# Delta layer: transposed outputs joined with block products on more tiles of the array, and a new order of squares, sums, norms and value copies

## What is computed

```python
qkvz = hidden_states @ w_qkvz.T
...
yc = jax.lax.conv_general_dilated(xc, conv_w[:, None, :], (1,), [(KCONV - 1, 0)], feature_group_count=CONV_DIM, dimension_numbers=('NCH', 'OIH', 'NCH'))
yc = jax.nn.silu(yc).transpose(0, 2, 1)
q, k, v = jnp.split(yc, [KEY_DIM, 2 * KEY_DIM], axis=-1)
...
q = q * jax.lax.rsqrt(jnp.sum(q * q, -1, keepdims=True) + L2_EPS)
k = k * jax.lax.rsqrt(jnp.sum(k * k, -1, keepdims=True) + L2_EPS)
...
def step(S, xs):
    qt, kt, vt, gt, bt = xs
    S = S * jnp.exp(gt)[..., None, None]
    kv = jnp.einsum('bhk,bhkv->bhv', kt, S)
    delta = (vt - kv) * bt[..., None]
    S = S + jnp.einsum('bhk,bhv->bhkv', kt, delta)
    o = jnp.einsum('bhk,bhkv->bhv', qt * scale, S)
    return (S, o)
...
xf = o.astype(jnp.float32) * jax.nn.silu(z.astype(jnp.float32))
var = jnp.mean(xf * xf, -1, keepdims=True)
xn = xf * jax.lax.rsqrt(var + NORM_EPS) * norm_weight
return xn.reshape(B, T, VALUE_DIM) @ w_out.T
```

## Time and profile before

| | |
|---|---|
| median of 3 runs | 2417.58 us (2417.31 to 2418.69) |
| profiled execution | 2418.08 us, its span from the first to the last instruction 2416.2 us |
| mean granted TensorE clock | 0.937 |
| busy in the span | PE 2096.6 us (87%), DVE 1845.9 us (76%), ACT 1462.5 us (61%), POOL 212.9 us (9%) |

### The profile page before, as it was taken

One profiled execution on the slowest core, in us unless ns is written; L12 is line 12 of the kernel. 1 busy time (PEld: TensorE's weight loads), 2 busy tenths in 40 slices (PEclk: granted clock), 3 DMA queues, 4 the chain that ended last, 5 costly groups with the idle time before them and its releaser, 6 DMA issues. The chain is left out here.

```text
span 2416.2 us, 41501 instructions
## 1 busy us (share of the span) xinstructions
PE 2096.6 (87%) x16485; PEld 1518.6 (63%) x16536; DVE 1845.9 (76%) x3313; ACT 1462.5 (61%) x2436; POOL 212.9 (9%) x163
## 2 busy tenths in 40 slices
PE   7997448999999999999976589999999996888854
PEld 4665325776666777776664355788888874555633
DVE  4776667888888888888877835478888776588697
ACT  3664255667777767676626631577777776455355
POOL 0000100011000000111100051000000000100313
PEclk8999768999999999999988799999999997999978
DMA  3000012322322222322216355311010000200001
GB/s 159 2 1 13 13 40 57 105 81 73 93 82 83 72 80 82 108 80 73 73 45 213 138 136 175 115 32 58 23 27 6 6 18 1 81 1 2 16 1 35
DMA packets 167063, 150.95 MB, mean 62 GB/s; under 512 B 118812, under 2 KB 146076, under 8 KB 158296
## 3 DMA queue, kind: packets, MB, share of 16 engines
q1 hardware_dynamic: 163032, 141.88, 18.5%
q0 software_dynamic: 3840, 6.43, 1.4%
HBM read 122.15 MB, written 26.11 MB: 61 GB/s over the span
## 5 line engine op out<-in xcount | busy, mean ns | idle before, releaser
L1607 DVE SCALAR_TENSOR_TENSOR ctx_chan<-l1a_raw,l1a_cw,ctx_chan 128x1024 f32<-128x1024 f32 x192 | 232.2, 1278 | 3.5 <-issue 3.5
L1213 PE MATMUL banks<-x_chan,l1a_wp 128*128 128x512 f32 x512 | 228.2, 599 | 3.4 <-ACT l1a_vt L1510 3.4
L1213 PEld LDWEIGHTS banks<-x_chan,l1a_wp 128*128 128x128 f32 x512 | 96.4, 191 | 125.9 <-issue 109.6
L1251 PE MATMUL banks<-l1a_wo,l1a_go 128*128 128x256 f32 x512 | 123.4, 396 | 15.2 <-DVE l1a_go L1836 8.5
L3172 PE MATMUL banks<-x_chan,more_weights_ahead 128*128 128x128 f32 x1024 | 123.6, 275 | 1.2 <-ACT l2a_kT L2699 1.2
L3172 PEld LDWEIGHTS banks<-x_chan,more_weights_ahead 128*128 128x128 f32 x1024 | 121.6, 192 | 3.9 <-ACT l2a_kT L2699 2.0
L1251 PEld LDWEIGHTS banks<-l1a_wo,l1a_go 128*128 128x128 f32 x512 | 100.0, 198 | 38.2 <-issue 21.6
L1200 POOL TENSOR_TENSOR l1a_al<-l1a_aT,l1a_outer 128x1024 f32<-128x1024 f32 x32 | 75.1, 2367 | 476.1 <-DVE l1a_aT L1667 476.1
L2712 ACT ACTIVATE l2a_masked<-l2a_masked,l2a_rowmax 128x128 f32<-128x128 f32 x256 | 98.9, 391 | 28.9 <-DVE l2a_rowmax L2925 28.9
L3208 PE MATMUL banks<-l2a_wo,l2a_oT 128*128 128x256 f32 x512 | 114.5, 382 | 0.0
L1221 PE MATMUL banks<-x_chan,l1a_wz 128*128 128x512 f32 x256 | 112.6, 593 | 0.0
(11 more groups left out here) (648 smaller groups left out, 5559.9 us busy)
## 6 DMA issues: line engine op xcount, KB each, us to landing
l1a_sq<-l1a_norm_mem SPq DMA_DIRECT2D x16, 1024.0 KB, 4.7
ctx_tok<-l1a_rows_mem SPq DMA_DIRECT2D x16, 1024.0 KB, 7.8
l1a_sq<-l1a_gnorm_mem SPq DMA_DIRECT2D x15, 1024.0 KB, 4.6
l1f_wgu<-in_l1f_wgu_dram SPq DMA_DIRECT2D x4, 1408.0 KB, 10.7
moe_sums<-l1x_zero SPq DMA_DIRECT2D x2, 2176.0 KB, 18.7
ctx_chan<-in_ctxT_dram SPq DMA_DIRECT2D x2, 2048.0 KB, 13.5
l1a_wp<-in_l1a_wp_dram SPq DMA_DIRECT2D x8, 512.0 KB, 5.6
l1f_wgu<-moe_sums SPq DMA_DIRECT2D x8, 512.0 KB, 8.1
```

What stands on the lines that cost most here:

```text
L1213: mm = MM(projected(i, u)[:, q * 512:(q + 1) * 512], wp[:, c, u * 128:(u + 1) * 128], g.xT[:, c, t0:t0 + 512], start=c == 0, stop=c == 1)
L1251: mm = MM(unit(h)[:, b * 256:(b + 1) * 256], go[:, HALF * h + 2 * b + r, :], wo[:, r, :], start=r == 0, stop=r == 1)
L1607: V.scalar_tensor_tensor(t, raw[:, u, :, j:j + S], cw[:, c, j:j + 1], t, ALU.mult, ALU.add).then_inc(s["conv_done" if step == 2 else "conv ...
```

## The change

Line numbers of the changed kernel are some 20 to 40 higher.

- `crossed` takes the place of `slot_half` for e1: the products go round all four tiles, and the second half's output lies with its two halves of partitions exchanged. ScalarE's `corrected` puts them back with two copies of 64 partitions.
- In `solve`, `upper` of quarter 1 writes partitions 64 to 127 and takes turns with quarter 0; `lower` of quarter 3 writes partitions 0 to 63 and takes turns with quarter 2. One signal follows each pair of quarters.
- `turn_values` for round i+1 stands in `solve` of round i, a half in each of two places, and the silu copies into `vt` at the end of ScalarE's round.
- `squares` go to `go2`, one unit at a time, right after that unit's silu, and these alternate with `z_out`. The sums go to bank 7 and stand ahead of `project_out(1)`; `norm_ln` and `norm_rs` stand ahead of the copies of `xT1`, and the second half of p1·xT0 waits for `norm_ln`.
- VectorE: from round 1 on, one `scale_gated`, then three steps for the key, three for the query, then the other `scale_gated`; the second `add` ahead of `xT2`, `weigh` ahead of the corrections. SyncE's `norms_in` waits for `normed`.

```diff
+        def sums_bank(i):
+
+            return 7 if i > 1 else 0
...
+        squares_kq = go2[:].rearrange("p (u b) n -> p u (b n)", u=2)
...
                 sp.wait_ge(s["norm_out"], 64 * i + 64)
+                if i > 1:
+                    sp.wait_ge(s["normed"], 2 * i - 2)
...
-            def turn_values(h):
+            def turn_values(i, h):
+                pe.wait_ge(s["conv_done"], 4 * i + 4)
+                if h == 0 and i < 2:
+                    pe.wait_ge(s["norm_ln"], i + 1)
+                if i > 1:
+                    pe.wait_ge(s["added"], 2 * i - 3 + h)
...
+            def crossed(lhsT, rhs):
+
+                for k in range(HALF):
+                    for row in range(2):
+                        p0 = 64 * row
+                        cols = slice(k * 64, k * 64 + 64)
+                        MM(ps[p0:p0 + 64, 4, cols], lhsT(p0, k), rhs(p0, k), start=True, stop=True)
+                        mm = MM(ps[64 - p0:128 - p0, 5, cols], lhsT(p0, k + HALF), rhs(p0, k + HALF), start=True, stop=True)
+                return mm
...
-                return MM(quarter(q)[0:64, k, :], xT2[0:64, slot, :], vt[0:64, slot, :], start=True, stop=True)
+                here = slice(64, 128) if q == 1 else slice(0, 64)
+                return MM(quarter(q)[here, k, :], xT2[0:64, slot, :], vt[0:64, slot, :], start=True, stop=True)
...
                 pe.wait_ge(s["xT2_out"], 2 * i + 1)
-                for q in range(2):
-                    for k in range(4):
-                        mm = upper(q, k)
-                    mm.then_inc(s["u_made"], 1)
+                for k in range(4):
+                    upper(0, k)
+                    mm = upper(1, k)
+                mm.then_inc(s["u_made"], 2)
+                if i + 1 < ROUNDS:
+                    turn_values(i + 1, 0)
...
-                for q in range(2, 4):
-                    pe.wait_ge(s["vr_made"], 4 * i + q + 1)
-                    for k in range(4):
-                        mm = lower(q, k)
-                    mm.then_inc(s["w_made"], 1)
+                if i + 1 < ROUNDS:
+                    turn_values(i + 1, 1)
+                pe.wait_ge(s["vr_made"], 4 * i + 4)
+                for k in range(4):
+                    lower(2, k)
+                    mm = lower(3, k)
+                mm.then_inc(s["w_made"], 2)
...
-                for h in range(2):
-                    slot_half(4, h, diagonal(al), within(x0)).then_inc(s["e1_made"], 1)
+                crossed(diagonal(al), within(x0)).then_inc(s["e1_made"], 2)
+                if i:
+                    next_sums()
                 previous_out(1)
-                if i:
-                    next_sums()
...
                 for h in range(2):
+                    if h and i and more:
+                        pe.wait_ge(s["norm_ln"], i + 2)
                     slot_half(6, h, within(p1), within(xT0)).then_inc(s["xT1_made"], 1)
...
+            def corrected(i, h):
+                act.wait_ge(s["e1_made"], 2 * i + h + 1)
+                if h == 0:
+                    A(heads(ec, h), half_out(2, h), ACT.Copy).then_inc(s["e1_out"], 1)
+                else:
+                    A(heads(ec, h)[0:64], half_out(2, h)[64:128], ACT.Copy)
+                    A(heads(ec, h)[64:128], half_out(2, h)[0:64], ACT.Copy).then_inc(s["e1_out"], 1)
...
+                if more and i:
+                    for u in range(2):
+                        for step in range(3):
+                            convolve(i + 1, 0, step, u)
```

More of the change, by code:

```diff
@@ L1387, in round_ @@
                     pe.wait_ge(s["tap"], 4 * i + 8)
-                for h in range(2):
-                    slot_half(4, h, diagonal(al), within(x0)).then_inc(s["e1_made"], 1)
-                previous_out(1)
+                crossed(diagonal(al), within(x0)).then_inc(s["e1_made"], 2)
                 if i:
                     next_sums()
+                previous_out(1)
                 pe.wait_ge(s["p1_made"], i + 1)
@@ L1433, in _ @@
             pe.wait_ge(s["rest_loaded"], 16 * 4)
+            for h in range(2):
+                turn_values(0, h)
             for i in range(ROUNDS):
@@ L1506, in round_ @@
                 if i:
-                    square(i - 1, 0)
-                for h in range(2):
-                    act.wait_ge(s["v_turned"], 2 * i + h + 1)
-                    A(heads(vt, h), slots(h), ACT.Silu).then_inc(s["v_out"], 1)
-                if i:
-                    square(i - 1, 1)
+                    for h in range(2):
+                        square(i - 1, h)
                     gate_norm(i - 1)
                 if more:
-                    for u in (0, 2, 1, 3):
+                    for n, u in enumerate((0, 2, 1, 3)):
+                        if i and n < 2:
+                            decay_exp(i + 1, n)
                         tap(i + 1, u)
-                if more:
+                if i and more:
+                    z_out(i, 0)
+                    silu(i + 1, 0)
+                    squares(i + 1, 0)
+                    z_out(i, 1)
+                    silu(i + 1, 1)
+                    squares(i + 1, 1)
+                else:
                     for h in range(2):
-                        decay_exp(i + 1, h)
+                        z_out(i, h)
                 for h in range(2):
-                    z_out(i, h)
+                    corrected(i, h)
                 if i and more:
-                    for u in range(2):
-                        silu(i + 1, u)
-                for h in range(2):
-                    act.wait_ge(s["e1_made"], 2 * i + h + 1)
-                    A(heads(ec, h), half_out(2, h), ACT.Copy).then_inc(s["e1_out"], 1)
-                if i and more:
-                    squares(i + 1)
                     norm_ln(i + 1)
+                    norm_rs(i + 1)
+                if i == 0:
+                    for h in range(2):
+                        decay_exp(1, h)
                 for h in range(2):
@@ L1564, in _ @@
                 silu(0, u)
-            squares(0)
+            for u in range(2):
+                squares(0, u)
             norm_ln(0)
@@ L1595, in link, with convolve @@
                 v.wait_ge(s["gate_chain"], count[0])
-            def convolve(i, first, step):
-                for u in range(first, first + 2):
+            def convolve(i, first, step, only=None):
+                for u in range(first, first + 2) if only is None else (only,):
                     if step == 0:
@@ L1602, in convolve @@
                     else:
-                        v.wait_ge(s["conv_chain"], 8 * i + 2 * first + 2 * (step - 1) + u % 2 + 1)
+                        v.wait_ge(s["conv_chain"], 8 * i + 2 * first + (2 * (u % 2) + step if i > 1 and first == 0 else 2 * (step - 1) + u % 2 + 1))
                     j = CONV - 2 - step
@@ L1764, in round_ @@
                 if i:
-                    for h in range(2):
-                        scale_gated(i - 1, h)
-                if more:
+                    scale_gated(i - 1, 0)
+                if more and i:
+                    for u in range(2):
+                        for step in range(3):
+                            convolve(i + 1, 0, step, u)
+                elif more:
                     for step in range(3):
@@ L1778, in round_ @@
                         convolve(i + 1, 2, step)
+                if i:
+                    add(i - 1, 1)
                 for h in range(2):
@@ L1781, in round_ @@
                     V.tensor_tensor(heads(xT2, h), half_out(3, h), heads(xT1, h), ALU.add).then_inc(s["xT2_out"], 1)
-                if i:
-                    add(i - 1, 1)
+                if more:
+                    for h in range(2):
+                        weigh(i + 1, h)
                 for q in range(4):
@@ L1786, in round_ @@
                     V.tensor_tensor(highs(vt, q), quarter(q)[64:128], highs(vt, q), ALU.add).then_inc(s["vr_made"], 1)
-                if more:
-                    for h in range(2):
-                        weigh(i + 1, h)
             v.wait_ge(s["gates_out"], 1)
```

54 lines of the change are left out of this document (27 added, 27 removed).

## The result

| | before | after |
|---|---|---|
| median of 6 runs each | 2416.60 us | 2389.67 us |
| ratio | | 0.9894, 95% interval 0.9873 to 0.9916 |
| profiled execution, its span | 2418.08 us, 2416.2 | 2388.50 us, 2386.6 |
| first to second key products (round 0) | 65.43 us | 67.24 us |
| a steady round, mean of 14 | 54.25 us | 52.34 us |

The forecast was 2388. One of the six runs after, 2442.74 us at a mean granted clock of 0.88, was a slow one; the ratio leaves it out, the median does not. The change touches nothing behind it, and what it touches ahead of it, from the layer's first matrix product on, took 39.50 before and 39.29 after.

What follows compares the result with a forecast made beforehand. The TensorE's work list was taken to bound each steady round. Saving 1.93 us 14 times (27.0), plus 1.5 in round 0 and 0.9 in the last, gave 29.4 off 2418.08: 2388.7, predicted as 2388 us, range 2380 to 2399.

Steps and rivals of the forecast that it cites:

- What bounds the kernel: Steady rounds: each is as long as the TensorE's list of work; what leaves it without becoming a wait gains 14 times.
- the sum: Whole kernel: 1.93 us a steady round, 27.0 over 14, plus 1.5 in round 0 and 0.9 in the last: 29.4.
- Two tiles and the transposes: Solve: paired groups halve to 0.93 and 0.94, transposes fill the places; uppers to key products 11.51 for 12.98, saving 1.47.
- Ahead of the solve: Steady round before the uppers: they start at 40.76 instead of 41.22, saving 0.46 a round, not 0.9.
- rival (c): ScalarE's cross-partition copies of e1 cost 1.0 each, 2397 us, or each shape change costs 0.27, 2398 us; chance 0.15.
- e1 and the squares: Ahead of the sums: e1 takes 1.0 for 2.01 on four tiles, but ScalarE's square holds the sums until 30.35.
- rival (a): e1 gains less on four tiles; with no gain a round saves 1.47, giving 2395.5 us; chance 0.18.
- ScalarE's slack: ScalarE before the first xT1 copy: ready at 36.0, wanted at 36.2, 0.2 us to spare, with copies at about 0.6.
- Round 0: First round: loses its value transposes in the same way as a steady round, saving 1.5 us.
- The last round: Final round: has no transposes to lose and gains only e1, 0.9 us.

Runs made afterwards that it cites:

- the second traces: Kernel before and changed kernel, both unchanged, each traced once more: 2413.02 us before, 2394.73 us changed.
- Pairs alone: Kernel before with only the uppers and lowers paired on two tiles, value transposes left ahead of the key products: 2425.32 us, steady round 54.22.

## Why the prediction was right, and where it was not

**What bounds the kernel** was read rightly: what leaves the TensorE's list in a steady round leaves the time, 14 times. The steady stretch went from 759.47 to 732.81 us (432.05 to 1191.52, then 434.17 to 1166.98): 26.7, and 26.0 between the second traces; the sum had 27.0.

**Two tiles and the transposes.** 11.63 for a forecast of 11.51. The groups of eight pairs took 1.03 and 1.02 to the next shape, for 0.93 plus 0.1. The forecast halved the lowers' 1.89 with the change of shape in it, so it had 0.94 where 1.02 was needed. Ahead of the solve the round gained 0.13 more than forecast (0.59 for 0.46); the two errors cancel, and that the round came out at 52.26 for 52.27 is luck to that extent. Pairs alone and the change without pairs show that the term belongs to both together. A change of shape, 1.02 less eight steps of 0.11, is 0.14 here, near the 0.13 taken from the earlier trace rows. Not all of it is the change: the last record of a group and the first of the next shape are 0.20 apart, but between uppers and across products, which have one shape, it is 0.17 in the kernel before. The Trainium skill, "TensorEngine Tiling (Array Packing)", section "Key Properties", says that a change of tiling mode drains the engine; the trace agrees that it costs something (0.20 where a step is 0.11), but not a record's whole 0.27, the price in rival (c).

**e1 and the squares.** 64 records start within 0.95, for 1.0; the sums start at 30.23, for 30.35, held by the square as forecast (VectorE's steps ended at 27.93 for 28.2, and silu and square took 0.15 longer from there). The records start 15 ns apart on average (0.95 / 63), those of one group of four about 7 (0.02 / 3). The Trainium skill, "TensorE: Matmul & The Clock Gate", section "Wait — 56ns, not 53.3ns?", states a floor of about 25 ns from start to start; taken across tiles, as the prediction did for its estimate of 1.6, the trace contradicts it, and rival (a) falls with it. Taken away one at a time, the pairs cost a round 1.72 and e1's four tiles 0.59, more together than the 1.94 gained, since the transposes in the solve cost time without the pairs.

**ScalarE's slack.** Rival (c)'s other half is out as well: the copies across partitions took 0.59.

**Round 0 is the step that failed.** The sum gave it 1.5 for the transposes, "in the same way" as a steady round. It lost 1.8, and 1.0 between the second traces. Of that, 0.7 and 0.3 is the run: the projections start that much later. The rest is mostly the order, where the forecast put the moved exponentials at nothing and left the clock out. From the projections to p1·xT0 the round became 1.2 and 1.9 shorter (28.79 for 30.00, 29.12 for 30.98). From there to the sums it became 2.7 and 2.9 longer: 1.3 is the longer wait, behind the table load that the exponentials force, and the rest stands where the 3.4 us at half clock lie on p1·xT0 (from 404.31) and no longer on e1 (from 399.78). Behind the sums the longer stretch at half clock costs 1.0, so that there only 0.3 was gained where 1.3 is gained without the move. Leaving the exponentials where they were would not have given the 1.5 either: two of the three traces with them back are still 0.7 to 1.4 longer than those of before, since e1 on four tiles then has the longer stretch at half clock. The rows that would have told were in reach: the forecast priced round 0 from a steady round's rows, though the earlier trace rows shows it at 53.36 of 63.50 busy and a clock of 0.85, which is a round that waits for others.

**The last round** and what follows it to the end of the layer gained 0.7 and 0.4 (80.35 to 79.69, 80.04 to 79.62) for a forecast of 0.9.

**The total.** By the layer the gain is 25.5 us in the first pair of traces (905.25 to 879.74) and 25.4 in the second, where the sum had 29.4. The median of before less 25.5 is 2391.1; the measured 2389.67 is 1.4 lower, within the spread of single runs. The first profiled execution is 29.6 shorter, the second pair (2413.02 and 2394.73) 18.3: what is over or under 25.5 lies in layers that the change doesn't touch, ahead of the first key products (366.62 to 366.93 us, then 364.08 to 368.94) and behind the layer. That the forecast missed the median by only 1.7 us is therefore partly luck; its steady term is not.

## What to carry to other kernels

When a chain of copies and corrections paces a stretch, making its products faster only opens holes; look for independent work of the same engine that fits them, and count both together. Price the first round of a loop from its own rows, its clock among them, and count a moved activation with the table load that it forces on the next one. An early result that seems to cost time on the busiest engine may be what keeps a transfer behind it off the path: look at its slack before moving it back.

## What the runs showed of the hardware

Four 64 x 64 tiles took a record each within 0.02 us; the next group of four followed after 0.11 and the others each 0.06 us or less (64 starts in 0.95), with each record 0.22 to 0.27 long. ScalarE's copies of 64 partitions to the other 64 cost 0.59, as copies in place do (0.57 to 0.60). In round 0 the granted clock was 0.50, the lower of its two levels, for 12.3 us after a wait of 4.05, and for 10.2 after one of 2.73:

```profile
413.50:423.70 10.20, 10.20 (x74) 8.45 (x76) 1.39 (x2) 6.10 (x8) 0.00 (x0) 0.50 0.26 90
```

```profile
415.95:428.25 12.30, 12.29 (x95) 9.97 (x96) 2.08 (x3) 6.71 (x9) 0.00 (x0) 0.50 0.37 148
```

The first fence is a window of the kernel before, the second of the changed one, with the columns of the earlier trace rows: the TensorE was busy throughout both, and a product there took about twice its time (the sums 1.93, in a steady round 1.06).
